# A Mamba and FFN kernel on one core: the DMA queue's engine gets an order of its own, and the lists of all engines are drawn anew

## The chip, the cores and the metric
One core of a Trainium2 chip (trn2). The core has five engines: PE (TensorE), DVE (VectorE), ACT (ScalarE), POOL (GpSimd) and SP (SyncE), which here only issues DMAs. The metric is the time of one execution on the device in microseconds.

## The reference, cut to what matters
Input is x, 8 rows of 1024 tokens with 256 channels. Everything is float32.

```python
def mamba(x, W_in, conv_w, conv_b, W_xproj, W_dt, b_dt, A_log, D_skip, W_out):
    xi, z = split(x @ W_in.T)                      # 512 channels each
    u = silu(causal_conv4(xi, conv_w) + conv_b)
    dt_r, B, C = split(u @ W_xproj.T)              # 16, 16, 16
    dt = softplus(dt_r @ W_dt.T + b_dt)
    A = -exp(A_log)                                # 512 x 16
    # for every channel c and state s, over the tokens of a row:
    #   h[t] = h[t-1] * exp(dt[t] * A) + dt[t] * u[t] * B[t];  y[t] = sum_s h[t] * C[t]
    y = (y + u * D_skip) * silu(z)
    return y @ W_out.T

def ffn(x, w_gate, w_up, w_down):                  # int weights / 127, hidden size 768
    return (silu(x @ w_gate.T) * (x @ w_up.T)) @ w_down.T

x = layernorm(x + mamba(x))
x = layernorm(x + ffn(x))
```

## The kernel before, in words
**Chunks.** The 8 rows of 1024 tokens are cut into 16 chunks of 512 tokens, one after the other; the second half of a row starts from the states that the first half left. In chunk k the core scans the states of chunk k. Beside that it does the *head* of chunk k + 1 (`xi`, convolution, `xproj`, `dt`) and the *tail* of chunk k - 1 (`out`, first normalisation, `x1T`, `gate`, `up`, `down`). The second normalisation and the store are those of chunk k - 2.

**The scan.** A chunk has 64 scans: 4 blocks of 128 channels by 16 states. They are grouped in 16 quads of 4. For each scan ACT makes a decay (`decay_step`, L641), POOL makes a drive for two scans at a time (`drive_unit`, L507: 32 a chunk, from `dtu` and `b_all`), DVE scans (L831). PE transposes the states (L1030, four groups per quad), ACT copies them out (`hT`, L648), and PE multiplies with the diagonals of C and sums (L1044, item `sum`). POOL makes the diagonals (`diag`, L515) from `c_col`. Buffers are few: 3 decays, 4 drives of two scans, 3 quads of states, 2 banks for transposes and 2 banks (`ring`) for all other products. `b_all` and `c_col` have one buffer each, in four parts (g = 0 to 3). A part of `b_all` is free for the next chunk after drives 25, 27, 29 and 31 of this one (counted from 0).

**The order.** Each engine runs its own program in order, and waits on semaphores. Beside the scan's own steps its items stand in a dictionary, `PE_SIDE`, `ACT_SIDE`, `DVE_SIDE`, `POOL_SIDE`. The key (q, j) is a slot: quad q, step j within it (0 to 3; on POOL, 0 and 1, one per drive). ACT's decays are 2 ahead of DVE's scans, and PE transposes in slot (q, j) what quad q - 1 left. Names that matter below: `xi`, `z`, `gate`, `up`: one product of 512 columns; `norm` 0 and 1: four ACT instructions that normalise `res` in place (L699), which need POOL's `std` 0 and 1; `heads` (L528): POOL clears or copies the three columns ahead of `xi` once the convolutions are done; `gate` on POOL: y times silu(z); `x1T`: the transposed input of the FFN; the block of items in ACT's slot (6, 0) needs another table of functions, so a table load stands ahead of it and another behind it (1.28 us each).

**SP.** SP's program has no dictionary. In chunk k it does, in this order: `load_res(k - 1)`; `store(k - 2)`, which waits for `a_o`, counted by `norm` 1; `spread_bc(k + 1)`, which waits for `a_dbl` (ACT's copy of `xproj`), writes B and C to a scratch tensor in memory, waits for that, and loads `c_col` in 16 small DMAs; `load_xt(k + 2)`; then four `load_b(g)`, each behind a wait for its drive. In chunks 0 and 1 there is no store. `b_all` has every row of B on all 128 partitions, 1 MB a part. `xt` and `res` of a chunk are 512 KB each.

Of the kernel before, what the change touches and what calls it, by code (L numbers as in the profile page):

```python
# [48 lines left out]


PE_SIDE = {
    (0, 1): [("xi", 0)], (0, 3): [("sum", 14), ("sum", 15)], (1, 0): [("turn", 3)], (1, 1): [("xi", 1)],
    (1, 2): [("out", 0, 0)], (2, 0): [("out", 0, 1)], (2, 2): [("out", 1, 0)], (3, 0): [("sum", 0)],
    (3, 2): [("out", 1, 1)], (4, 0): [("sum", 1)], (4, 2): [("xi", 2)],
    (5, 0): [("xi", 3), ("z", 0), ("sum", 2), ("sum", 3), ("z", 1), ("z", 2), ("z", 3)],
    (5, 2): [("x1T", 0), ("x1T", 1)], (6, 0): [("turn", 0), ("gate", 0), ("gate", 1)], (6, 2): [("gate", 2)],
    (7, 0): [("sum", 4)], (7, 3): [("up", 0)], (8, 0): [("sum", 5)], (8, 2): [("xproj", 0)],
    (9, 0): [("dt", 0), ("sum", 6), ("sum", 7)], (9, 2): [("up", 1), ("up", 2)], (10, 0): [("gate", 3)],
    (10, 2): [("up", 3)], (11, 0): [("dt", 1), ("sum", 8), ("sum", 9)],
    (11, 2): [("turn", 1), ("gate", 4), ("gate", 5)], (12, 0): [("up", 4)], (12, 1): [("up", 5)],  # L60
    (12, 3): [("sum", 10), ("sum", 11)], (13, 1): [("down", 0, 0), ("turn", 2)], (13, 3): [("down", 0, 1)],
    (14, 1): [("sum", 12)], (14, 3): [("down", 1, 0), ("down", 1, 1)], (15, 3): [("sum", 13)],
}
ACT_SIDE = {
# [16 lines left out]
}  # L81
DVE_SIDE = {
    (1, 2): [("skip", 3)], (4, 2): [("r1", 0)], (5, 0): [("r1", 1)],
    (6, 0): [("conv", 0, 0), ("conv", 0, 1), ("conv", 0, 2), ("conv", 1, 0), ("conv", 1, 1), ("conv", 1, 2), ("conv", 2, 0), ("conv", 2, 1), ("conv", 2, 2), ("conv", 3, 0), ("conv", 3, 1), ("conv", 3, 2), ("skip", 0)],
    (6, 1): [("gs", 0)], (7, 1): [("gs", 1)], (7, 2): [("gs", 2)], (8, 3): [("hid", 0)], (9, 3): [("hid", 1)],
    (10, 0): [("hid", 2)], (10, 3): [("gs", 3), ("hid", 3)], (11, 2): [("skip", 1)], (11, 3): [("gs", 4)],
    (12, 1): [("gs", 5)], (13, 0): [("hid", 4), ("hid", 5)], (14, 1): [("skip", 2)], (14, 3): [("r2", 0)],
    (15, 3): [("r2", 1)],
}
POOL_SIDE = {  # L90
    (2, 1): [("diag", 1), ("gate", 3)], (5, 0): [("diag", 2)], (5, 1): [("diag", 3)], (6, 0): [("std", 0)],
    (6, 1): [("heads", 0)], (7, 0): [("dtu", 1)], (12, 0): [("dtu", 0)], (12, 1): [("std", 1)],
    (13, 0): [("gate", 0)], (15, 1): [("gate", 1), ("gate", 2), ("diag", 0)],
}
PROLOGUE = [("xi", 0), ("xi", 1), ("xi", 2), ("xi", 3), ("xproj", 0), ("dt", 0), ("dt", 1)]
PE_FIRST = PE_LAST = PE_SIDE
ACT_FIRST = ACT_LAST = ACT_SIDE
# [61 lines left out]
def wait(eng, sem, value):  # L159

    if not isinstance(value, int) or value > 0:
        eng.wait_ge(sem, value)
# [39 lines left out]
def banks_of(item):  # L202

    what, i, *part = item
    if what == "dt":
        return [(what, 2 * i), (what, 2 * i + 1)]
    if what == "sum" or what.startswith("end_") or part and part[0] > 0:
        return []
    return [(what, i)]
# [15 lines left out]
def products_in_order(chunks):  # L225

    order = [(what, i, 0) for item in PROLOGUE for what, i in banks_of(item)]
    for c in range(chunks):
# [7 lines left out]
def mamba_ffn(nc, x, xT, W_inT, conv_w, conv_b, W_xT, W_dtT, b_dt, A_log, D_skip, W_outT,  # L236
# [5 lines left out]
    with ExitStack() as ctx:  # L242
        def sb(name, shape, dt=F32):
            return ctx.enter_context(nc.sbuf_tensor(name, shape, dt))
# [27 lines left out]
        xt = sb("xt", [P, 2, DH, T])  # L272
        res = sb("res", [P, 2, TB, DM])
        xi = sb("xi", [P, CB, KW - 1 + T])
        u = sb("u", [P, 2, CB, T])
        dt = sb("dt", [P, 2, CB, T])
        dtu = sb("dtu", [P, CB, T])
        sz = sb("sz", [P, CB, T])
# [6 lines left out]
        hT = sb("hT", [P, HTS, T])  # L285
        yt = sb("yt", [P, T])
        yg = sb("yg", [P, CB, T])
        hid = sb("hid", [P, HB - CB, T])
# [105 lines left out]
        def _(eng):  # L394

            def load_xt(k):
                eng.dma_start(xt[:, k.parity, :, :],
                              xT[:, bass.ds(k.tokens(), T)].rearrange("(a p) t -> p a t", p=P))\
                   .then_inc(l_xt[k.parity], 16)
# [20 lines left out]
            def load_b(g):  # L420
                src = bc_dram[4 * g:4 * g + 4, :].rearrange("(o n) t -> o n t", o=1)
                eng.dma_start(b_all[:, 4 * g:4 * g + 4, :], src.to_broadcast([P, 4, T]))\
                   .then_inc(l_b[g], 16)

            def store(k):
                wait(eng, a_o, k.count(4, 4))
                eng.dma_start(out[bass.ds(k.tokens(), T), :].rearrange("(a p) d -> p a d", p=P),
                              res[:, k.parity, :, :]).then_inc(st_out, 16)

            def load_res(k):  # L430
                wait(eng, st_out, k.count(16, -16))
                eng.dma_start(res[:, k.parity, :, :],
                              x[bass.ds(k.tokens(), T), :].rearrange("(a p) d -> p a d", p=P))\
                   .then_inc(l_res, 16)

            def chunk(k, tail, head, more, late=True):
                if tail:
                    load_res(k + -1)
                if late:
                    store(k + -2)  # L440
                if head:
                    spread_bc(k + 1)
                if more:
                    if tail:
                        wait(eng, p_up, k.count(6, 0))
                    else:
                        wait(eng, p_z, k.count(4, 4))
                    load_xt(k + 2)
                if head:
                    for g in range(4):  # L450
                        wait(eng, g_dr, k.count(32, 24 + 2 * g + 2))
                        load_b(g)

            load_xt(Chunk(0, 0))

# [10 lines left out]
            for half in range(2):  # L466
                chunk(Chunk(0, half), half == 1, True, True, False)
            for row in range(1, ROWS - 1):
                for half in range(2):
                    chunk(Chunk(row, half), True, True, True)  # L470
            for half in range(2):
                chunk(Chunk(ROWS - 1, half), True, half == 0, False)
            kl = Chunk(ROWS - 1, 1)
            load_res(kl)
            store(kl + -1)
            for done, blocks in ((2, slice(0, 2)), (3, slice(2, 3)), (4, slice(3, 4))):
                eng.wait_ge(e_o, done)
# [541 lines left out]
        def _(eng):  # L1019
# [273 lines left out]
            eng.wait_ge(l_in[0], 16)  # L1293
            for what, i in PROLOGUE:
                if (what, i) == ("xi", 1):
# [51 lines left out]
```

## Time and profile before

| | us |
|---|---|
| median of 3 runs | 2083.94 (2083.55 to 2084.12) |
| the profiled execution | 2083.41 |
| its span | 2081.6 |
| PE busy | 1773.4 (85%) |
| DVE busy | 1617.7 (78%) |
| ACT busy | 1617.6 (78%) |
| POOL busy | 1470.6 (71%) |
| mean granted clock of PE | 0.929 of full speed |

The span is from the first to the last instruction in the profile; 1.8 us of the execution lie around it. Busy shares are means over the whole span. PE's weight loads are a group of their own (PEld) and run beside its matmuls. SP's queue entries are issues of DMAs: time between them is SP waiting.

### The profile page before, as it was taken

To read this page: it belongs to the slowest core of one execution; us is meant where nothing else is said; L and a number is where in the kernel's file an instruction comes from. 1 tells how busy PE (TensorE), PEld (TensorE's weight loads), DVE (VectorE), ACT (ScalarE), POOL (GpSimd) and SP (SyncE) were. 2 spreads that over 40 slices of the span, in tenths; PEclk is the share of its full clock that TensorE was granted. 3 is DMA by queue.
4 is the path that set the end of the run, shared out by engine and by line. 5 is a ranking of instruction groups with operands and counts; after the bars stand their busy time and mean duration, and the time that the engine had idled before them with its cause. 6 is when DMAs were issued, how large, how long until landed. Compare 5 with 4: busy or idle time off the path is not lost.

```text
span 2081.6 us, 40418 instructions
## 1 busy us (share of the span) xinstructions
PE 1773.4 (85%) x15806; PEld 1260.1 (61%) x15806; DVE 1617.7 (78%) x1877; ACT 1617.6 (78%) x2792; POOL 1470.6 (71%) x853
## 2 busy tenths in 40 slices
PE   6779998796988969789697896979969699696897
PEld 3556766564665656556565674656756567565676
DVE  5889997795977959689595995959958599586784
ACT  6799897695977959679596895959959599595871
POOL 5788886785857958579584895848868487685860
PEclk8899999898998989999899998989989899898999
DMA  6030301203012030120302103030030300303000
GB/s 183 3 102 3 103 2 13 102 2 113 2 15 100 1 114 1 33 83 2 114 1 63 53 2 114 2 82 33 2 114 1 109 6 13 102 2 104 1 22 21
DMA packets 172146, 100.61 MB, mean 48 GB/s; under 512 B 139538, under 2 KB 158738, under 8 KB 163892
## 3 DMA queue, kind: packets, MB, share of 16 engines
q1 hardware_dynamic: 171956, 98.02, 16.3%
q8 instruction: 126, 2.06, 0.4%
q14 instruction: 64, 0.52, 0.1%
HBM read 88.56 MB, written 9.44 MB: 47 GB/s over the span
## 4 chain that ended last, share of the span: by engine, by line
PE 49%; issue 16%; POOL 11%; ACT 10%; DVE 8%; SPq 4%; DMA 2%; POOLq 0%; ACTq 0%; DVEq 0%
PE ring L1051 14%; PE tp L1030 14%; POOL drive L507 8%; PE yb L1044 8%; PE ring L1149 4%; DVE h L831 4%; PE ring L1125 3%; DVE u L852 3%; SPq L417 3%; ACT hT L648 3%; ACT decay L641 2%; ACT res L699 2%; POOL diag_c L515 2%; ACT u L668 1%; PE ring L1107 1%
## 5 line engine op out<-in xcount | busy, mean ns | idle before, releaser
L507 POOL TENSOR_TENSOR drive<-dtu,b_all 128x1024 f32<-128x1024 f32 x511 | 1201.9, 2378 | 233.0 <-issue 164.0
L641 ACT ACTIVATE decay<-dt,a_neg 128x512 f32<-128x512 f32 x1024 | 688.5, 699 | 263.9 <-DVE h L831 260.7
L831 DVE TENSOR_TENSOR_SCAN h<-decay,h,drive 128x512 f32<-128x512 f32 x512 | 623.5, 1271 | 153.1 <-issue 135.8
L831 DVE TENSOR_TENSOR_SCAN h<-decay,drive 128x512 f32<-128x512 f32 x512 | 594.2, 1212 | 164.8 <-POOL drive L507 121.6
L1030 PE MATMUL tp<-ident,h 128*128 128x128 f32 x4096 | 579.9, 284 | 117.1 <-ACT hT L648 110.8
L1030 PEld LDWEIGHTS tp<-ident,h 128*128 128x128 f32 x4096 | 476.0, 145 | 308.0 <-ACT hT L648 183.8
L648 ACT ACTIVATE hT<-tp 128x512 f32<-128x512 f32 x1024 | 570.9, 601 | 108.7 <-PE tp L1030 107.9
L1051 PE MATMUL ring<-xt,w_in 128*128 128x512 f32 x512 | 261.3, 652 | 142.6 <-DMA xt<-in_xT 140.3
L1044 PE MATMUL yb<-hT,diag_c 128*32 128x128 f32 x8192 | 279.7, 288 | 0.0
L1044 PEld LDWEIGHTS yb<-hT,diag_c 128*32 128x32 f32 x8192 | 228.1, 115 | 49.5 <-issue 38.0
L1051 PEld LDWEIGHTS ring<-xt,w_in 128*128 128x128 f32 x512 | 97.9, 204 | 246.0 <-issue 232.0
L515 POOL TENSOR_TENSOR diag_c<-of_token,c_col 128x512 f32<-128x512 f32 x64 | 67.3, 1052 | 161.0 <-DMA c_col<-bc_scratch 159.4
L1051 PE MATMUL ring<-xt,w_u 128*128 128x512 f32 x360 | 167.8, 595 | 0.0
L1051 PE MATMUL ring<-xt,w_g 128*128 128x512 f32 x360 | 164.4, 593 | 0.0
L852 DVE SCALAR_TENSOR_TENSOR u<-xi,cw,u 128x512 f32<-128x512 f32 x189 | 144.7, 787 | 14.0 <-ACT xi L659 9.6
L1125 PE MATMUL ring<-w_out,yg 128*128 128x256 f32 x480 | 115.4, 384 | 27.4 <-POOL yg L521 27.4
L1149 PE MATMUL ring<-w_d,xi 128*128 128x256 f32 x480 | 113.5, 379 | 0.0
L1125 PEld LDWEIGHTS ring<-w_out,yg 128*128 128x128 f32 x480 | 87.0, 191 | 39.7 <-issue 30.3
L528 POOL TENSOR_TENSOR spare_g<-eps,minus 128x4 f32<-128x4 f32 x17 | 3.4, 200 | 138.7 <-DVE u L852 128.0
L1051 PEld LDWEIGHTS ring<-xt,w_g 128*128 128x128 f32 x360 | 63.7, 190 | 57.4 <-issue 57.4
L1149 PEld LDWEIGHTS ring<-w_d,xi 128*128 128x128 f32 x480 | 87.7, 190 | 10.1
L1051 PEld LDWEIGHTS ring<-xt,w_u 128*128 128x128 f32 x360 | 62.5, 190 | 51.0 <-issue 50.2
(124 smaller groups left out, 1426.1 us busy)
## 6 DMA issues: line engine op xcount, KB each, us to landing
b_all<-bc_scratch SPq DMA_DIRECT2D x63, 1024.0 KB, 9.1
xt<-in_xT SPq DMA_DIRECT2D x16, 512.0 KB, 5.0
res<-in_x SPq DMA_DIRECT2D x16, 512.0 KB, 13.6
out<-res SPq DMA_DIRECT2D x15, 512.0 KB, 3.0
c_col<-bc_scratch SPq DMA_DIRECT2D x256, 2.0 KB, 2.4
bc_scratch<-dbl SPq DMA_DIRECT2D x32, 32.0 KB, 2.4
b_all<-bc_scratch SPq DMA_DIRECT2D x2, 512.0 KB, 4.3
w_g<-in_w_gT SPq DMA_DIRECT2D x1, 768.0 KB
```

Of the source, the lines that this page charges most:

```text
L417: eng.dma_start(c_col[s:P - 3 + s:4, g, :], bc_dram[N + 4 * g + s, :].rearrange("(b t) -> t b", t=TS), allow_slow_non_contiguous=True).the ...
L507: tt(drive[:, j % 4, :, :], src, b_all[:, n:n + 2, :], ALU.mult).then_inc(g_dr, 1)
L515: tt(diag_c[:, g, :, :], mask, col, ALU.mult).then_inc(g_dc, 1)
L641: act(decay[decay_slot(k.parity, i)][:, :], dt[:, k.parity, cb, :], ACT.Exp, scale=a_neg[:, cb, n:n + 1]).then_inc(a_da, 1)
L648: act(hT[:, (64 * k.index + g) % HTS, :], tp[g % 2][:, :], ACT.Copy).then_inc(a_ev, 1)
L831: nc.vector.tensor_tensor_scan(h[:, h_slot(k.parity, q), at:at + T, i % 4], decay[decay_slot(k.parity, i)][:, :], drive[:, (i // 2) % 4, i ...
L852: stt(u[:, k.parity, cb, :], xi[:, cb, tap:tap + T], cw[:, cb, tap:tap + 1], u[:, k.parity, cb, :], ALU.mult, ALU.add).then_inc(v_conv, 1)
L1030: last = nc.tensor.transpose(tp[g % 2][:, b * P:(b + 1) * P], h[:, h_slot(k.parity, q), t0:t0 + TS, :].rearrange("p t s -> p (t s)"), iden ...
L1044: last = mm(yb[b * TS:(b + 1) * TS, f * P:(f + 1) * P], diag_c[:, q % 4, 4 * f + b, :], hT[:, (64 * k.index + g) % HTS, b * P:(b + 1) * P] ...
L1051: last = mm(bank, lhsT, rhs, start=i == 0, stop=i == len(pairs) - 1)
L1125: last = mm(bank(k, "out", i)[:, half * DM:(half + 1) * DM], yg[:, c, tb * P:(tb + 1) * P], w_out[:, c, :], start=c == 0, stop=c == CB - 1)
L1149: last = mm(bank(k, "down", i)[:, half * DM:(half + 1) * DM], hidden_block(m)[:, tb * P:(tb + 1) * P], w_d[:, m, :], start=m == 0, stop=m ...
```

## The change
SP gets an order of its own for a chunk, `SP_ORDER`. The spread of B and C comes first, then three `b_all` loads, then the store, the load of `res`, the fourth `b_all` load and `xt`. `load_res` is now that of chunk k itself, at this place in chunk k, in place of that of k - 1 at the start of the chunk; its wait is for the store just ahead of it. The dictionaries of PE, ACT, DVE and POOL are drawn anew: same items, other slots. `POOL_FIRST`, the first chunk's own list of POOL, stays, as do the lists of the end.

```diff
 PE_SIDE = {
-    (0, 1): [("xi", 0)], (0, 3): [("sum", 14), ("sum", 15)], (1, 0): [("turn", 3)], (1, 1): [("xi", 1)],
-    (1, 2): [("out", 0, 0)], (2, 0): [("out", 0, 1)], (2, 2): [("out", 1, 0)], (3, 0): [("sum", 0)],
-    (3, 2): [("out", 1, 1)], (4, 0): [("sum", 1)], (4, 2): [("xi", 2)],
-    (5, 0): [("xi", 3), ("z", 0), ("sum", 2), ("sum", 3), ("z", 1), ("z", 2), ("z", 3)],
-    (5, 2): [("x1T", 0), ("x1T", 1)], (6, 0): [("turn", 0), ("gate", 0), ("gate", 1)], (6, 2): [("gate", 2)],
-    (7, 0): [("sum", 4)], (7, 3): [("up", 0)], (8, 0): [("sum", 5)], (8, 2): [("xproj", 0)],
...
+    (0, 3): [("xi", 0), ("sum", 14), ("sum", 15), ("xi", 1), ("turn", 3)], (1, 1): [("xi", 2)],
+    (1, 2): [("out", 0, 0)], (2, 0): [("out", 0, 1)], (2, 2): [("xi", 3)], (3, 0): [("sum", 0), ("sum", 1)],
+    (3, 2): [("out", 1, 0)], (4, 0): [("out", 1, 1)], (5, 0): [("sum", 2)], (5, 2): [("z", 0), ("z", 1)],
+    (6, 0): [("z", 2), ("z", 3), ("sum", 3), ("x1T", 0), ("x1T", 1)], (6, 1): [("turn", 0), ("sum", 4)],
+    (6, 3): [("xproj", 0), ("gate", 0), ("gate", 1)], (7, 1): [("gate", 2)], (7, 3): [("sum", 5)],
...
 ACT_SIDE = {
-    (13, 0): [("hT", 48), ("y", 2)], (13, 2): [("hT", 49)], (13, 3): [("hT", 50)],
-    (14, 2): [("hT", 51), ("hT", 52), ("hT", 53)], (14, 3): [("hT", 54), ("norm", 1)],
...
+    (6, 0): [("sz", 0), ("sz", 1), ("norm", 0), ("hT", 19), ("sz", 2), ("u", 0), ("sz", 3), ("u", 1), ("y", 0), ("x1T", 0), ("u", 2), ("hT", 20), ("hT", 21), ("x1T", 1), ("u", 3)],
+    (6, 3): [("xproj", 0), ("hT", 22), ("hT", 23), ("tanh", 0)],
...
+    (13, 0): [("y", 2), ("hT", 48), ("hT", 49)], (13, 1): [("hT", 50), ("hT", 51)], (13, 3): [("norm", 1)],
...
 POOL_SIDE = {
-    (2, 1): [("diag", 1), ("gate", 3)], (5, 0): [("diag", 2)], (5, 1): [("diag", 3)], (6, 0): [("std", 0)],
-    (6, 1): [("heads", 0)], (7, 0): [("dtu", 1)], (12, 0): [("dtu", 0)], (12, 1): [("std", 1)],
-    (13, 0): [("gate", 0)], (15, 1): [("gate", 1), ("gate", 2), ("diag", 0)],
+    (1, 1): [("diag", 1)], (3, 0): [("gate", 3)], (4, 0): [("diag", 2)],
+    (6, 1): [("std", 0), ("diag", 3), ("heads", 0)], (7, 1): [("dtu", 1)], (10, 0): [("std", 1)],
+    (11, 0): [("dtu", 0)], (13, 1): [("gate", 0)], (14, 0): [("gate", 1)], (15, 0): [("gate", 2)],
+    (15, 1): [("diag", 0)],
 }
+SP_ORDER = [("spread", 0), ("bload", 0), ("bload", 1), ("bload", 2), ("store", 0), ("res", 0), ("bload", 3), ("xt", 0)]
...
-            def chunk(k, tail, head, more, late=True):
-                if tail:
-                    load_res(k + -1)
-                if late:
+            def item(k, what, i, tail, head, more, late):
+                if what == "res":
+                    load_res(k)
+                if what == "store" and late:
                     store(k + -2)
-                if head:
+                if what == "spread" and head:
                     spread_bc(k + 1)
-                if more:
+                if what == "xt" and more:
                     if tail:
                         wait(eng, p_up, k.count(6, 0))
                     else:
                         wait(eng, p_z, k.count(4, 4))
                     load_xt(k + 2)
-                if head:
-                    for g in range(4):
-                        wait(eng, g_dr, k.count(32, 24 + 2 * g + 2))
-                        load_b(g)
+                if what == "bload" and head:
+                    wait(eng, g_dr, k.count(32, 24 + 2 * i + 2))
+                    load_b(i)
+
+            def chunk(k, tail, head, more, late=True):
+                for what, i in SP_ORDER:
+                    item(k, what, i, tail, head, more, late)
...
-            load_res(kl)
             store(kl + -1)
```

DVE's list changes too: the twelve convolution steps, all in slot (6, 0) before, now stand as five in (5, 3) and seven in (6, 0).

## Rows read from the trace of the kernel before

**Rows 1.** The waits: engine and line, awaited; us in total, times, longest.
```profile
POOL drive L507 <- issue: 164.0, 13, 13.1
POOL diag_c L515 <- DMA c_col<-bc_scratch: 159.4, 13, 12.8
PE ring L1051 <- DMA xt<-in_xT: 140.3, 12, 12.7
...
PE ring L1125 <- POOL yg L521: 27.4, 14, 2.7
```

**Rows 2.** The waits of SP's own queue.
```profile
SPq L427 <- ACT res L699: 1589.6, 15, 112.4
```

**Rows 3.** Timeline of ACT at a boundary: start, us, instructions, idle before.
```profile
991.87 2.06 ACT L699 ACTIVATE res<-res,shift,rstd 128x256 f32<-128x256 f32 x4
```

**Rows 4.** Timeline of SP at the same boundary.
```profile
993.96 0.39 SPq L427 DMA_DIRECT2D out<-res  x1
...
997.37 10.73 SPq L417 DMA_DIRECT2D c_col<-bc_scratch  x16
1008.14 0.62 SPq L397 DMA_DIRECT2D xt<-in_xT  x1
1008.81 2.13 SPq L422 DMA_DIRECT2D b_all<-bc_scratch  x4
```

**Rows 5.** Timeline of POOL at the same boundary.
```profile
987.37 2.51 POOL L521 TENSOR_TENSOR yg<-yg,sz 128x512 f32<-128x512 f32 x2
1001.85 1.04 POOL L515 TENSOR_TENSOR diag_c<-of_token,c_col 128x512 f32<-128x512 f32 x1 [11.96 <-DMA c_col<-bc_scratch]
1015.79 14.00 POOL L507 TENSOR_TENSOR drive<-dtu,b_all 128x1024 f32<-128x1024 f32 x6 [12.89 <-issue]
```

**Rows 6.** Timeline of PE at the same boundary.
```profile
1013.33 3.75 PE L1051 MATMUL ring<-xt,w_in 128*128 128x512 f32 x4 [11.00 <-DMA xt<-in_xT]
1020.74 1.97 PE L1030 MATMUL tp<-ident,h 128*128 128x128 f32 x8 [3.66 <-ACT hT L648]
```

**Rows 7.** Timeline of PE at the boundary from chunk 1 to chunk 2.
```profile
251.74 1.88 PE L1051 MATMUL ring<-xt,w_in 128*128 128x512 f32 x4
253.46 1.04 PE L1030 MATMUL tp<-ident,h 128*128 128x128 f32 x8
```

**Rows 8.** Busy time in one stretch: PE, PEld, DVE, ACT, POOL, PE's clock, DMA share, GB/s.
```profile
1010.00:1018.00 8.00, 3.75 (x4) 1.17 (x4) 0.00 (x0) 0.00 (x0) 2.21 (x1) 0.50 0.99 386
```

**Rows 9.** Timeline of SP at the boundary from chunk 1 to chunk 2.
```profile
205.19 11.04 SPq L417 DMA_DIRECT2D c_col<-bc_scratch  x16
...
229.00 8.68 SPq L422 DMA_DIRECT2D b_all<-bc_scratch  x4
```

**Rows 10.** Busy time as in rows 8, of two whole chunks.
```profile
184.90:291.70 106.80, 105.19 (x985) 75.37 (x984) 99.98 (x117) 98.93 (x172) 90.51 (x49) 1.00 0.19 52
...
993.96:1122.29 128.33, 109.95 (x985) 77.79 (x985) 98.88 (x117) 101.15 (x176) 91.67 (x52) 0.92 0.16 47
```

**Rows 11.** POOL's spare_g instruction of heads: ns min/median/max, first and last start.
```profile
L528 POOL TENSOR_TENSOR spare_g<-eps,minus x17: 198/200/204, 3.7 to 1834.1; 128x4 f32<-128x4 f32 x17
```

**Rows 12.** DVE's scans in the page's costliest groups: busy, mean ns, idle before.
```profile
L831 DVE TENSOR_TENSOR_SCAN h<-decay,drive 128x512 f32<-128x512 f32 x512 | 594.2, 1212 | 164.8 <-POOL drive L507 121.6
```

**Rows 13.** Timeline of POOL at the boundary from chunk 1 to chunk 2.
```profile
232.46 4.87 POOL L507 TENSOR_TENSOR drive<-dtu,b_all 128x1024 f32<-128x1024 f32 x2 [1.15 <-DVE h L831]
...
241.85 9.35 POOL L507 TENSOR_TENSOR drive<-dtu,b_all 128x1024 f32<-128x1024 f32 x4
```

**Rows 14.** DMA issues: count, KB each, median us from issue to landing.
```profile
out<-res SPq DMA_DIRECT2D x15, 512.0 KB, 3.0
```

**Rows 15.** Timeline of ACT: the table loads around the block of slot (6, 0).
```profile
1054.31 1.28 ACT L673 ACT_TABLE_LOAD   x1
...
1065.76 1.28 ACT L641 ACT_TABLE_LOAD   x1
```

**Rows 16.** Timeline of PE: the xproj product.
```profile
1077.84 1.95 PE L1088 MATMUL ring<-u,w_x 128*64 128x256 f32 x16
```

More of the change, by code:

```diff
@@ L58 @@
[L58 to L62, printed above, removed]
+    (0, 3): [("xi", 0), ("sum", 14), ("sum", 15), ("xi", 1), ("turn", 3)], (1, 1): [("xi", 2)],
@@ new lines @@
+    (1, 2): [("out", 0, 0)], (2, 0): [("out", 0, 1)], (2, 2): [("xi", 3)], (3, 0): [("sum", 0), ("sum", 1)],
+    (3, 2): [("out", 1, 0)], (4, 0): [("out", 1, 1)], (5, 0): [("sum", 2)], (5, 2): [("z", 0), ("z", 1)],
+    (6, 0): [("z", 2), ("z", 3), ("sum", 3), ("x1T", 0), ("x1T", 1)], (6, 1): [("turn", 0), ("sum", 4)],
+    (6, 3): [("xproj", 0), ("gate", 0), ("gate", 1)], (7, 1): [("gate", 2)], (7, 3): [("sum", 5)],
+    (8, 1): [("up", 0)], (8, 3): [("dt", 0), ("sum", 6), ("sum", 7)], (9, 1): [("up", 1), ("up", 2)],
@@ L63 @@
+    (9, 3): [("gate", 3)], (10, 1): [("up", 3)], (10, 3): [("sum", 8)], (11, 1): [("dt", 1)],
+    (11, 3): [("sum", 9), ("sum", 10)], (12, 1): [("gate", 4), ("gate", 5)], (12, 2): [("turn", 1)],
+    (12, 3): [("up", 4), ("up", 5), ("sum", 11)], (13, 1): [("turn", 2)],
+    (13, 3): [("down", 0, 0), ("down", 0, 1)], (14, 1): [("sum", 12)], (14, 3): [("down", 1, 0)],
+    (15, 1): [("down", 1, 1)], (15, 3): [("sum", 13)],
 }
 ACT_SIDE = {
[16 rows of a table removed]
[16 rows of a table added]
 }
 DVE_SIDE = {
-    (1, 2): [("skip", 3)], (4, 2): [("r1", 0)], (5, 0): [("r1", 1)],
@@ L84 @@
[L84 to L87, printed above, removed]
@@ L88 @@
-    (15, 3): [("r2", 1)],
+    (1, 2): [("skip", 3)], (3, 2): [("r1", 0)], (5, 0): [("r1", 1)],
+    (5, 3): [("conv", 0, 0), ("conv", 0, 1), ("conv", 0, 2), ("conv", 1, 0), ("conv", 1, 1)],
+    (6, 0): [("conv", 1, 2), ("conv", 2, 0), ("conv", 2, 1), ("conv", 2, 2), ("conv", 3, 0), ("conv", 3, 1), ("conv", 3, 2)],
+    (6, 1): [("skip", 0)], (7, 1): [("gs", 0)], (7, 3): [("gs", 1), ("gs", 2)], (8, 2): [("hid", 0)],
+    (9, 2): [("hid", 1)], (9, 3): [("hid", 2)], (10, 2): [("gs", 3)], (11, 0): [("hid", 3)],
@@ L89 @@
+    (12, 0): [("gs", 4), ("gs", 5), ("skip", 1)], (12, 3): [("hid", 4), ("hid", 5)], (13, 2): [("skip", 2)],
+    (14, 2): [("r2", 0)], (15, 3): [("r2", 1)],
 }
 POOL_SIDE = {
-    (2, 1): [("diag", 1), ("gate", 3)], (5, 0): [("diag", 2)], (5, 1): [("diag", 3)], (6, 0): [("std", 0)],
-    (6, 1): [("heads", 0)], (7, 0): [("dtu", 1)], (12, 0): [("dtu", 0)], (12, 1): [("std", 1)],
-    (13, 0): [("gate", 0)], (15, 1): [("gate", 1), ("gate", 2), ("diag", 0)],
+    (1, 1): [("diag", 1)], (3, 0): [("gate", 3)], (4, 0): [("diag", 2)],
```

27 rows, old and new, of the table ACT_SIDE are left out of this document.

## The prediction
> **What bounds the kernel now.** I read the waits first, then the timelines of the engines around the largest of them, then the busy time of whole chunks. The list of waits has three groups that come once per chunk, and their counts and sizes match: POOL's `diag_c` waits 12 us for `c_col` from the DMA, 13 times; right after it POOL's drive sits idle another 12.6 us, 13 times ("issue", a wait that the profile does not attribute); PE's first input product waits 11.7 us for `xt`, 12 times [rows 1]. The queue's own waits say who holds them: SP stands at line 427, the store, waiting for ACT's second normalisation, 15 times and 1590 us in all [rows 2]. Line 427 is ahead of everything else that SP does in a chunk.
>
> At one boundary it reads so. ACT's four `res` instructions end at 993.93 [rows 3]; SP issues the store at 993.96 and only then the rest: 16 `c_col` issues in 10.7 us, `xt` at 1008.14, the four `b_all` from 1008.81 [rows 4]. POOL has finished the chunk's last drive at 987.4 and its gates at 989.9, gets `c_col` at 1001.85 and `b_all` at 1015.79 [rows 5]. So POOL loses 12.0 + 12.9 = 24.9 us. DVE and ACT run dry behind it, PE waits for `xt` until 1013.33 and is back on transposes only at 1020.74; the product then takes 3.75 us, where it takes 1.88 in the other boundary [rows 6, 7], because the granted clock of that stretch is 0.50, the lower of the two levels [rows 8].
>
> The same kernel shows a boundary without this. Chunks 0 and 1 have no store, so the spread of chunk 1 for chunk 2 went out at 205.19 and the `b_all` loads at 229.00, as drives set them free [rows 9]. From chunk 1's `heads` (184.9) to chunk 2's (291.7) it takes 106.8 us, with PE 105.19 us busy (98.5%) at a granted clock of 1.00, DVE 99.98, ACT 98.93, POOL 90.51; a later chunk takes 128.33 with PE 109.95 at 0.92 [rows 10]. The `heads` of chunks 2 and 14 (the last of 17) are at 291.7 and 1834.1, 12 periods: 128.53 us each [rows 10, 11]. This pair is the core of the forecast: without the SP stall PE is the bound, at 105.2 us a chunk, and the work of all engines fits in 106.8.
>
> **The change, part by part.** (1) *SP's order.* The spread now waits for `a_dbl` alone, which ACT gives in slot (6, 3). Its issues take about 14 us (10.7 for `c_col`, some 3.4 for the scratch writes and their landing [rows 4]), and are done long before POOL's (15, 1). The loads 0 to 2 wait for drives 25, 27 and 29. The two POOL waits, 24.9 us, go. None of this is extra work: the number of DMAs is the same, only their order changes.
>
> (2) *What now stands behind the store.* The store waits for `norm` 1, then `load_res` waits for the store's landing, and behind these two stand the fourth `b_all` load and `xt`. Which is late next? In the old chunk ACT's norm ended 6.6 us after POOL's last drive (993.93 against 987.4 [rows 3, 5]), from slot (14, 3). It moves to (13, 3), four decays earlier; each decay follows a scan of about 1.2 us [rows 12], so I put its end 1.7 us after the last drive. I lay that on the boundary without stall, where the last drive ended at 237.3 [rows 13]: norm 239.0, store issued 0.4 later, landed 3.0 after that [rows 14], 242.4. Behind it `res`, `b_all` and `xt` are 2.1 MB; at the 386 GB/s that the loads reached [rows 8] 5.4 us, and the store's 3.0 us less its own 1.4 us of bytes leaves 1.6 us of latency. With half a microsecond of issue, `xt` lands at about 250.0. The product that needs it started at 251.74 there, in slot (0, 1) [rows 7]; the new lists put it at (0, 3), two groups of transposes (0.5 us each [rows 7]) further on. Taking 252 to 253, 2 to 3 us are to spare: cost 0. If the cover is gone the cost is the lateness itself, on PE, 13 times. The last `b_all` is first needed in POOL's seventh drive, 14 us into the chunk: no cost.
>
> One rule speaks against this step. The Trainium skill, "DMA: Bandwidth & Descriptors", gives under "Anatomy of one DMA" a fixed 2.0 us and bytes over 436 GB/s, and under "Bandwidth" a limit of some 358 GB/s between one core and its memory. By the first `xt` would land at 242.9 + 2.0 + 4.8 = 249.7, by the second at 250.8. It makes a wait for a completed write ahead of loads cost its full latency, and the trace bears out the size of that (3.0 us [rows 14]); both results are still ahead of 252.
>
> (3) *The lists.* The work per engine is unchanged: PE 105.2, ACT 98.9 plus the second norm's 2.06 [rows 3], DVE 100, POOL 90.5. So the floor of a chunk is 105.2, and what counts is the idle time of PE. Two new places: the `xi` products now come early, so the block of Silu work in ACT's (6, 0) finds PE with little in stock. ACT's block took 12.7 us from its table load to the end of the load back [rows 15]. PE has in (6, 0) to (6, 3) four products (1.7 each), `xproj` (1.9), four groups of transposes, `x1T`, a turn and two sums (about 5 together): 13.8 us [rows 7, 16]. The last `gate` waits for ACT's copy of `xproj`, which stands behind the block and three decays, about 17.5 us after the start: 3.7 us of PE idle. Second, `out` 0 waits in (1, 2) for POOL's `gate` 3, which moves from after the sixth to after the seventh drive; PE already waits 2.0 us a time there (27.4 over 14 [rows 1]), and I reckon 1.9 for it and for `xi` 2 behind ACT's copy of `xi` 1. If PE had no backlog anywhere, a chunk would be 105.2 + 3.7 + 1.9 = 110.8. If it always had, 105.2. The old lists without a stall made 106.8, the nearest row. PE has the most work of the four engines (105.2 against at most 101), so it runs behind the others for much of a chunk and can fill a wait from its backlog; I count half of the two waits: 105.2 + 2.8 = **108.0 us**. Ends for the range: 105.5 and 112.
>
> **Sum.** Twelve periods: 12 x (128.53 - 108.0) = 246.4. The thirteenth boundary, into the last chunk, has no `xt` and stalls about 2.2 us less: 18.3. The period from chunk 1 to 2 gets 1.2 longer (108.0 against 106.8). Chunk 0, the last chunk and the end keep their work; I count 0 with 4 us either way, since the last chunk is already a chunk with little to fill it. 2083.4 (the profiled execution's own time, 0.5 below the median of 2083.94) less 263.5: **1820 us**.
>
> **The rivals.**
> *The new lists fit worse.* PE idle grows beyond both waits counted, say a chunk of 112: 12 x 16.5 + 14.3 - 5.2 = 207, 1876 us. For it: ACT has 101 us of work in the chunk with both normalisations, and its long block stands where the `xi` stock is gone. Against: no engine has over 105.2, and lists of this kind reached 106.8. Chance 0.11.
> *A new wait takes the place of the old.* `xt` arrives late behind store, `res` and `b_all`. If norm ends as late as before (6.6 us after the last drive) it lands near 255, 2 to 3 us late; with PE's restart at the low clock after it, 5 us a boundary, chunks of 113: 12 x 15.5 + 13.3 - 6.2 = 193, 1890 us. Chance 0.07.
> *Slower than before.* Same place, with a longer chain: `norm` needs POOL's `std` in (10, 0), the store needs `norm`, `res` needs the store, PE's `xi` needs `xt`. It decides when `xt` is later than PE's need by more than 128.5 - 108 = 20.5 us a chunk, when the store would have to be some 23 us later than reckoned; at 24 us, 1820 + 13 x 24 = 2132 us. Nothing in the rows delays it so; `std` 1 has its input since the chunk's start. Chance 0.02.
> *The change doesn't do what it says.* The POOL idle labelled "issue" might be another limit; but it ends as `b_all` lands, and at the boundary where SP was free the drive goes on at 241.85, 4.5 us after the last one with two gates and `diag_c` between [rows 5, 13]. No gain, 2083: chance 0.01.
> *The clock.* PE nearly always busy could be granted less than now. The unstalled chunk ran at 1.00 for all of its 106.8 us [rows 10], so I add nothing; the mean should rise from 0.93.
>
> **How the numbers follow.** The forecast (chunks of 105.5 to 110.5, 1784 to 1855) has 0.79; worse lists 0.11, late `xt` 0.07, slower 0.02, no change 0.01. A range of 1788 to 1866 leaves out the last three, half of the worse lists and a little at the lower end. About 0.2% (4 us) is what a measurement of this kernel can tell from no change. Faster 0.97, within 0.2% 0.01, slower 0.02.
>
> **What would show it right or wrong.** `heads` 106 to 111 us apart; no wait of `diag_c` for `c_col`, no idle of the drive over 2 us at the boundary; SP's `c_col` issues in mid chunk and its long wait now ahead of `b_all` or the store; PE's clock near 1.00 outside the first and last chunk; PE over 95% busy; short PE waits for ACT around the Silu block. Wrong: a wait of PE's input product for `xt` of over 1 us each chunk (second rival), or ACT more than 97% busy with PE under 94% (first).

## The result, and the profile after

| | before | after |
|---|---|---|
| median, us | 2084.03 (4 runs) | 1803.8 (4 runs, 1801.26 to 1804.67) |
| ratio, 95% interval | | 0.8654 (0.8639 to 0.8669) |
| span of the profiled execution, us | 2081.6 | 1803.0 |
| mean granted clock of PE | 0.929 | 0.983 |

The forecast was 1820 us with a range of 1788 to 1866. The page of the changed kernel, its busy times and the shares of the chain that ended last:

```profile
span 1803.0 us, 40418 instructions
PE 1727.5 (96%) x15806; PEld 1230.6 (68%) x15806; DVE 1603.5 (89%) x1877; ACT 1620.4 (90%) x2792; POOL 1473.2 (82%) x853
...
PE 73%; DVE 9%; ACT 8%; issue 6%; POOL 4%; SPq 0%; DMA 0%; POOLq 0%; ACTq 0%; DVEq 0%
```

The same shares in the kernel before:

```profile
PE 49%; issue 16%; POOL 11%; ACT 10%; DVE 8%; SPq 4%; DMA 2%; POOLq 0%; ACTq 0%; DVEq 0%
```

SP and the DMAs, 6% of the chain before, are gone from it. In the list of waits the three that came once per chunk [rows 1] have no successor. What the same instructions still wait for is other engines, little at a time (total us, times, longest); the first row is the longest total among the scan's own waits, the last one is PE's wait for `gate` 3 on POOL, which the forecast had counted in every chunk:

```profile
DVE h L836 <- ACT decay L646: 87.9, 58, 4.7
POOL drive L512 <- DVE h L836: 71.9, 41, 11.0
...
POOL diag_c L520 <- PE yb L1049: 9.2, 14, 0.7
...
PE ring L1130 <- POOL yg L526: 6.5, 2, 4.7
```

SP's own waits, where the 1590 us at the store [rows 2] are now spread over several places, the largest one for `a_dbl` in mid chunk:

```profile
SPq L407 <- ACT dbl L686: 831.5, 16, 61.1
SPq L425 <- POOL drive L512: 451.0, 47, 17.2
SPq L430 <- ACT res L704: 188.8, 15, 100.0
SPq L435 <- DMA out<-res: 39.8, 14, 3.5
```

One boundary in SP's timeline (L425 is a `b_all` load, L430 the store, L435 `res`, L400 `xt`, L420 `c_col`; compare [rows 4]):

```profile
990.23 0.39 SPq L430 DMA_DIRECT2D out<-res  x1
993.16 0.38 SPq L435 DMA_DIRECT2D res<-in_x  x1
993.58 0.51 SPq L425 DMA_DIRECT2D b_all<-bc_scratch  x1
994.13 0.43 SPq L400 DMA_DIRECT2D xt<-in_xT  x1
1049.68 0.79 SPq L407 DMA_DIRECT2D bc_scratch<-dbl  x2
1051.62 10.80 SPq L420 DMA_DIRECT2D c_col<-bc_scratch  x16
1079.52 14.26 SPq L425 DMA_DIRECT2D b_all<-bc_scratch  x3
```

The same boundary on POOL, where [rows 5] had 12.0 and 12.9 us of idle:

```profile
990.26 2.39 POOL L512 TENSOR_TENSOR drive<-dtu,b_all 128x1024 f32<-128x1024 f32 x1
993.35 1.05 POOL L520 TENSOR_TENSOR diag_c<-of_token,c_col 128x512 f32<-128x512 f32 x1 [0.70 <-PE yb L1049]
994.36 7.02 POOL L512 TENSOR_TENSOR drive<-dtu,b_all 128x1024 f32<-128x1024 f32 x3
```

On PE the first `xi` product starts with no wait and at full clock (1.88 us where [rows 6] have 3.75):

```profile
1004.40 1.88 PE L1056 MATMUL ring<-xt,w_in 128*128 128x512 f32 x4
```

Two whole chunks in busy time (PE, PEld, DVE, ACT, POOL, clock, DMA share, GB/s), to set against [rows 10]:

```profile
937.80:1044.70 106.90, 106.16 (x1004) 75.59 (x1008) 98.61 (x117) 101.68 (x177) 91.78 (x52) 1.00 0.20 56
1044.70:1151.30 106.60, 105.47 (x979) 74.70 (x972) 99.34 (x117) 100.97 (x175) 91.83 (x52) 1.00 0.20 57
```

The `heads` of the first and last full period, as [rows 11]: the last one starts at 1578.2, that of chunk 2 at 297.49 in POOL's timeline.

```profile
L533 POOL TENSOR_TENSOR spare_g<-eps,minus x17: 200/202/752, 3.7 to 1578.2; 128x4 f32<-128x4 f32 x17
```

(1578.2 - 297.49) / 12 = 106.73 us a chunk, where it was 128.53. So the 278.6 us of the span come in three parts: 12 x 21.8 = 261.6 from the twelve periods; 22.7 from the last boundary to the end (1803.0 - 1578.2 = 224.8, before 2081.6 - 1834.1 = 247.5); and 5.8 lost up to the `heads` of chunk 2 (297.49 against 291.68). All of that loss lies before the `heads` of chunk 1 (190.74 against 184.88); from there to chunk 2 both kernels take the same, 106.75 and 106.80 us.

### The profile page after: what moved, and what is told of

Same layout as the page of the kernel before. It is cut to its first block, busy times and chain, and to the rows that moved or that the text cites. A ratio compares the mean times of both kernels' runs of the same rounds, so it can differ in the third digit from the quotient of the medians.

```text
span 1803.0 us, 40418 instructions
## 1 busy us (share of the span) xinstructions
PE 1727.5 (96%) x15806; PEld 1230.6 (68%) x15806; DVE 1603.5 (89%) x1877; ACT 1620.4 (90%) x2792; POOL 1473.2 (82%) x853
## 4 chain that ended last, share of the span: by engine, by line
PE 73%; DVE 9%; ACT 8%; issue 6%; POOL 4%; SPq 0%; DMA 0%; POOLq 0%; ACTq 0%; DVEq 0%
PE ring L1056 25%; PE tp L1035 20%; PE yb L1049 11%; PE ring L1130 6%; DVE h L836 6%; PE ring L1154 4%; ACT hT L653 3%; POOL drive L512 3%; PE ring L1112 2%; PE ring L1093 2%; ACT L646 1%; ACT L693 1%; ACT decay L646 1%; DVE u L857 1%; ACT dt L693 1%
## 5 line engine op out<-in xcount | busy, mean ns | idle before, releaser
L653 ACT ACTIVATE hT<-tp 128x512 f32<-128x512 f32 x1024 | 562.7, 602 | 60.2 <-PE tp L1035 57.8
L1035 PE MATMUL tp<-ident,h 128*128 128x128 f32 x4096 | 566.1, 280 | 34.5 <-ACT hT L653 32.2
L1035 PEld LDWEIGHTS tp<-ident,h 128*128 128x128 f32 x4096 | 465.6, 143 | 189.7 <-ACT hT L653 82.6
L1049 PE MATMUL yb<-hT,diag_c 128*32 128x128 f32 x8192 | 265.6, 276 | 2.3 <-ACT hT L653 2.2
L1049 PEld LDWEIGHTS yb<-hT,diag_c 128*32 128x32 f32 x8192 | 212.9, 110 | 64.5 <-issue 47.5
L1056 PE MATMUL ring<-xt,w_in 128*128 128x512 f32 x512 | 241.7, 607 | 1.6 <-ACT dt L693 0.9
L1056 PEld LDWEIGHTS ring<-xt,w_in 128*128 128x128 f32 x512 | 91.6, 193 | 89.6 <-issue 84.6
L526 POOL TENSOR_TENSOR yg<-yg,sz 128x512 f32<-128x512 f32 x63 | 80.7, 1282 | 0.0
```

Source lines behind the costliest of these rows:

```text
L526: tt(yg[:, cb, :], yg[:, cb, :], sz[:, cb, :], ALU.mult).then_inc(g_y, 1)
L653: act(hT[:, (64 * k.index + g) % HTS, :], tp[g % 2][:, :], ACT.Copy).then_inc(a_ev, 1)
L1035: last = nc.tensor.transpose(tp[g % 2][:, b * P:(b + 1) * P], h[:, h_slot(k.parity, q), t0:t0 + TS, :].rearrange("p t s -> p (t s)"), iden ...
L1049: last = mm(yb[b * TS:(b + 1) * TS, f * P:(f + 1) * P], diag_c[:, q % 4, 4 * f + b, :], hT[:, (64 * k.index + g) % HTS, b * P:(b + 1) * P] ...
L1056: last = mm(bank, lhsT, rhs, start=i == 0, stop=i == len(pairs) - 1)
```

## The experiments

All ratios are to the kernel before, run beside it on the same chip. The period is read as above, from the `heads` of chunks 2 and 14 in each trace.

| run | us | ratio, 95% interval | heads, chunk 2 and 14 | us a chunk |
|---|---|---|---|---|
| before | 2084.03 | | 291.68, 1834.1 | 128.5 |
| the change | 1803.8 | 0.8654 (0.8639 to 0.8669) | 297.49, 1578.2 | 106.7 |
| e1, SP's order, old lists | 1860.56 | 0.8927 (0.8914 to 0.8941) | 293.58, 1631.0 | 111.5 |
| e2, old SP, new lists | 2055.6 | 0.9863 (0.9849 to 0.9878) | 296.52, 1812.2 | 126.3 |
| e3, store last, old lists | 1799.02 | 0.8631 (0.8617 to 0.8645) | 294.12, 1573.0 | 106.6 |
| e4, spread first, old lists | 1915.44 | 0.9195 (0.9179 to 0.9212) | 293.37, 1679.4 | 115.5 |
| e5, the change, store last | 1803.92 | 0.8649 (0.8637 to 0.8661) | 296.72, 1577.5 | 106.7 |
| e6, the change, old first chunk | 1800.73 | 0.8634 (0.8623 to 0.8646) | 293.95, 1574.7 | 106.7 |
| c1, the change again | 1803.74 | 0.8649 (0.8637 to 0.8661) | 297.68, 1578.4 | 106.7 |
| c2, e3 again | 1799.65 | 0.8631 (0.8619 to 0.8643) | 291.64, 1570.9 | 106.6 |
| e9, xt later, 2 copies | 1848.78 | 0.8866 (0.8837 to 0.8896) | 293.93, 1617.8 | 110.3 |
| e10, xt later, 5 copies | 1962.84 | 0.9404 (0.9388 to 0.9419) | 311.15, 1736.1 | 118.7 |
| e11, gate half | 1806.88 | 0.8665 (0.8652 to 0.8677) | 298.42, 1579.8 | 106.8 |
| e12, store from ACT, old lists | 1807.47 | 0.8663 (0.865 to 0.8676) | 291.42, 1579.6 | 107.3 |

### Which part of the change brings it: e1 to e4

**e1** is the changed kernel with the four dictionaries of before.

```diff
-PE_SIDE = {  (0, 3): [("xi", 0), ("sum", 14), ...        # likewise ACT, DVE, POOL
+PE_SIDE = {  (0, 1): [("xi", 0)], (0, 3): [("sum", 14), ...
```

> SP's new order with the four dictionaries of before. Theory A (the gain is SP's order; the old lists without a stall made 106.8 us a chunk, as from chunk 1 to 2 in the kernel before): POOL's two boundary waits go. But the old norm 1 in slot (14, 3) ends 6.6 us after POOL's last drive and the old first xi product in (0, 1) wants xt about 14.4 us after it; store landing 3.0, issues about 1.3 and the 7.7 us to landing that xt has in the changed kernel make 18.6, so xt is some 4 us late and a restart of PE is added: 106.8 + 5 = 112 us a chunk, about 1870 us. Theory B (the lists carry a large part of the gain, at least a third): over 1900 us.

1860.56 us and 111.5 us a chunk: theory A, to a half per cent. This is also the prediction's second rival, met with the old lists: 4.9 us a chunk over e3, for the 5 that were put on a late `xt`. The lateness of `xt` is there; the wait is 3.3 us a time (expected 4):

```profile
PE ring L1054 <- DMA xt<-in_xT: 40.0, 12, 4.5
```

and at one boundary PE starts after it at the lower clock again, 3.75 us for the product that takes 1.88 otherwise:

```profile
1031.71 3.75 PE L1054 MATMUL ring<-xt,w_in 128*128 128x512 f32 x4 [3.48 <-DMA xt<-in_xT]
```

**e2** is the kernel before with the new dictionaries, SP untouched.

> SP as before (residual, store, spread, xt, four b_all), with the new dictionaries. Theory A: the stall stays, but norm 1 comes from slot (13, 3), some 4.9 us earlier against POOL's last drive than from (14, 3), so each of 13 boundaries stalls that much less: about 2084 - 13 x 5 = 2020 us, POOL still waiting about 8 us for c_col and then for b_all. Theory B: the new lists hold a good part of the gain by themselves, under 1960 us.

Neither number came. The lists alone bring 28 us. `diag_c` does wait 6.0 us less each time (81.6 over 13, before 159.4 over 13), which is what norm 1's earlier slot should give, but most of that is lost again on PE. Its waits:

```profile
POOL diag_c L517 <- DMA c_col<-bc_scratch: 81.6, 13, 7.5
PE ring L1053 <- DMA xt<-in_xT: 67.9, 12, 6.8
...
PE ring L1127 <- POOL yg L523: 59.5, 14, 6.6
PE ring L1118 <- ACT yt L666: 54.1, 14, 13.0
```

The two last rows have grown: `out` waits 4.3 us a time for `yg`, 2.0 in [rows 1], and `turn` 3.9 us for `yt`. In the new lists the first `xi` product stands ahead of the last two sums, so whatever waits for the sums (`yt`, `turn`, the skip, `gate` 3, `out`) now also waits for `xt`. That reading is from the order of the items and the two rows; no run moved `xi` alone, so it is not shown.

**e3** is the kernel before with one edit.

```diff
 def chunk(k, tail, head, more, late=True):
     if tail:
         load_res(k + -1)
-    if late:
-        store(k + -2)
     if head:
         spread_bc(k + 1)
...
             load_b(g)
+    if late:
+        store(k + -2)
```

> The kernel before with one edit: the store moves from ahead of the spread to the end of SP's chunk. No new lists, the residual stays first. Theory A: nothing needed soon stands behind the store any more, chunks take the 106.8 us of the unstalled one plus up to 1.5 for the second normalisation: 1800 to 1825 us. Theory B (the new lists are needed): over 1850 us.

1799.02 us, just under theory A's window of 1800 to 1825, and no slower than the whole change. So the gain needs neither the new lists nor the new place of the residual; it needs the store out of the way. SP's timeline of one chunk: the spread in mid chunk, `xt` and the four parts of B as drives release them, then a wait of 6 us for the store that nobody else stands behind.

```profile
1058.43 11.89 SPq L417 DMA_DIRECT2D c_col<-bc_scratch  x16
1083.21 0.40 SPq L397 DMA_DIRECT2D xt<-in_xT  x1
1083.65 8.70 SPq L422 DMA_DIRECT2D b_all<-bc_scratch  x4
1098.55 0.39 SPq L427 DMA_DIRECT2D out<-res  x1
1102.40 0.38 SPq L432 DMA_DIRECT2D res<-in_x  x1
```

**e4** moves only the spread ahead of the store; `xt` and B's parts stay behind it.

```diff
+    if head:
+        spread_bc(k + 1)
     if late:
         store(k + -2)
-    if head:
-        spread_bc(k + 1)
     if more:
```

> The kernel before with the spread of B and C ahead of the store, but xt and the four b_all loads still behind it. Splits the stall in its parts. Theory A (two stalls in series, c_col and then b_all): c_col is there in time, xt and b_all are issued 1.6 us after the end of norm 1, so drives restart about 14 us after the last one where they did after 28.4, and after 4.5 in the boundary without stall: about 116 us a chunk, 1925 us, no wait of diag_c for c_col, and a drive idle of 8 to 10 us each boundary. Theory C (c_col alone is what holds the boundary, b_all and xt are hidden behind it): about 1815 us.

115.5 us a chunk for 116 expected: two stalls in series, about 13 us of the 22 a chunk from C's columns and 9 from B's parts and `xt`. `diag_c` no longer waits for a DMA, and the drive still does:

```profile
1043.62 1.05 POOL L515 TENSOR_TENSOR diag_c<-of_token,c_col 128x512 f32<-128x512 f32 x1 [1.11 <-PE yb L1044]
1055.35 13.97 POOL L507 TENSOR_TENSOR drive<-dtu,b_all 128x1024 f32<-128x1024 f32 x6 [10.68 <-issue]
```

### Whether it is the order on one queue: e12

**e12** leaves SP's order alone and takes the stores off it.

```diff
 def normalise(k, norm):                    # on ACT
     for tb in range(TB):
         act(res[:, k.parity, tb, :], ...).then_inc((a_x1, a_o)[norm], 1)
+    if norm:
+        wait(eng, a_o, k.count(4, 4))
+        eng.dma_start(out[bass.ds(k.tokens(), T), :]..., res[:, k.parity, :, :]).then_inc(st_out, 16)
...
 def chunk(k, tail, head, more, late=True):  # on SP
     if tail:
         load_res(k + -1)
-    if late:
-        store(k + -2)
...
-            store(kl + -1)
```

> The kernel before with nothing of SP's order changed but the stores taken off it: ACT issues each store itself, right after its second normalisation. Old lists. Theory A (what cost the time was only that the spread and all behind it stood behind a wait for norm 1 on one queue): the same gain as from the store at the end, 1798 to 1812 us, ACT's issue of about half a microsecond a chunk hidden. Theory I (the loads collide with the store's transfer, wherever it is issued): over 1850 us.

1807.47 us, theory A. The store's transfer at its old place in the order, right behind norm 1, costs nothing that shows; what cost was the wait in SP's program ahead of everything else. The issue on ACT's queue:

```profile
1098.92 2.06 ACT L696 ACTIVATE res<-res,shift,rstd 128x256 f32<-128x256 f32 x4
1101.02 0.38 ACTq L700 DMA_DIRECT2D out<-res  x1
```

One part of the expectation missed: the issue isn't hidden. A chunk takes 107.3 us where e3 and c2 take 106.6. In ten of the twelve periods the granted clock is 1.00 and a chunk takes 107.0 us on average, half a microsecond more. That is about what the issue costs ACT, which goes from the start of norm 1 to its next decay in 2.5 us where it took 2.0 in e3. In the two others the clock is 0.98 and a chunk takes 108.9, and these make the rest.

### What is left at the boundary: e5, e9, e10

**e5**: `SP_ORDER` ends with the fourth `b_all` load, `xt`, store, `res`.

> The changed kernel with the store and the residual moved behind the fourth b_all and xt. Theory A (PE is the bound at 106.7 us a chunk, and xt already lands about 2 us ahead of its use): no change, 1800 to 1806 us. Theory D (the wait for the store's landing ahead of xt still costs something each chunk): at least 1 us a chunk less, under 1792 us.

No change: 1803.92 us, and 1803.74 for the changed kernel run beside it (c1).

**e9 and e10** put two and five copies of 128 KB in memory, each waited for, ahead of every `xt` load.

```diff
+    for _ in range(2):                     # e10: 5
+        eng.dma_start(pad[:, :], x[0:P, :]).then_inc(st_pad, 16)
+        pads[0] += 16
+        eng.wait_ge(st_pad, pads[0])
     load_xt(k + 2)
```

> The changed kernel with two small copies in memory (128 KB each, each waited for, some 2 us) ahead of every xt load. In the changed kernel xt is issued at 888.27, lands 7.7 us later and is used at 897.93: some 2 us to spare. Theory A (that is all the cover there is): 14 boundaries are 2 to 3 us late, 1803.8 + 28 to 42 = 1832 to 1846 us, and PE waits for xt appear. Theory G (PE's backlog or a shorter landing absorbs it): under 1812 us.

> The same with five copies ahead of every xt load, some 10 us. Theory A (lateness counts one for one once the 2 us are used, and PE restarts at the lower clock): 8 us late plus 1 to 3 us for the clock at 14 boundaries, 1930 to 1960 us, granted clock down to about 0.95. Theory G (half of it is absorbed): under 1890 us. This prices the second rival of the prediction, a late xt.

Both landed a little above theory A's windows, because the copies take SP longer than the 2 us each that I put. One alone does land 2.3 to 2.4 us after its issue, but the first of them is issued behind `res` and the `b_all` part in flight and lands after 6.9 us (both in e10, from 1077.95 on). SP's timeline of e9, then of e10:

```profile
1010.84 0.51 SPq L427 DMA_DIRECT2D b_all<-bc_scratch  x1
1011.39 7.31 SPq L454 DMA_DIRECT2D pad_scratch<-in_x  x2
1020.50 0.38 SPq L402 DMA_DIRECT2D xt<-in_xT  x1
```

```profile
1077.95 14.57 SPq L454 DMA_DIRECT2D pad_scratch<-in_x  x5
1094.32 0.38 SPq L402 DMA_DIRECT2D xt<-in_xT  x1
```

The issue of `xt` moves by 9.1 and 16.4 us. But with `res` and the `b_all` part no longer in flight ahead of it, `xt` lands 3.7 us after its issue, not 7.7, so it is 5.1 and 12.4 us later. Chunks grow by 3.6 and 12.0 us. PE's waits, e9 and e10 (the 35.8 are over 13, 2.8 us each; the 129.7 over 14, 9.3 each):

```profile
PE ring L1062 <- DMA xt<-in_xT: 35.8, 13, 5.0
```

```profile
PE ring L1062 <- DMA xt<-in_xT: 129.7, 14, 10.9
```

So about 2 to 3 us of lateness are covered (5.1 less 2.8, 12.4 less 9.3), and beyond that a microsecond costs a microsecond, plus 0.8 (e9) and 2.7 us (e10) a chunk. In e9 the granted clock accounts for the 0.8: six of the twelve periods ran at 1.00 and took 109.3 us on average, 2.6 over the changed kernel; the other six ran at 0.98 and took 111.3. In e10 the late product itself runs at a granted clock of 0.50 (1098 to 1101 in its trace), and the mean of the execution is 0.946. Theory G is out.

### Where the first two chunks lose: e6, c1, c2

**e6** gives the first chunk the old lists of PE, ACT and DVE; `PE_FIRST`, `ACT_FIRST` and `DVE_FIRST` are the dictionaries of before.

> The changed kernel, with PE's, ACT's and DVE's lists of before in the first chunk alone. The changed kernel reaches the heads of chunk 2 at 297.49 us where the one before is at 291.68, the only place where it lost. Theory A (the new lists leave the first chunk, with POOL's list unchanged, worse matched): 3 to 6 us come back, 1798 to 1801 us. Theory E (the loss is in the change-over to the second chunk, whose lists are then still the new ones): within 2 us of the changed kernel, and heads of chunk 2 still near 297.

> The changed kernel as it is, on the same chip as the other runs of this call: 1801 to 1806 us under every theory.

> The kernel before with the store at the end of SP's chunk, on the same chip as the changed kernel. Theory A (both are bound by PE in the steady chunks, and differ by the 3 to 6 us of the first two chunks): 1797 to 1801 us, 3 to 6 below the changed kernel. Theory F (the first difference of 4.8 us was one between chips): within 1.5 us of it.

e6 takes 1800.73 us (1800.47 to 1801.19), c1 beside it 1803.74 (1803.38 to 1804.69): 3.0 us back, and the `heads` of chunk 2 come 3.7 us earlier. The loss sits between the `heads` of chunk 0 and of chunk 1. That stretch takes 104.3 to 104.8 us in the five runs with the new lists and `xt` in time, 99.6 to 101.8 in the six with the old lists, and 101.0 in e6. So the first chunk's lists carry most of the loss, perhaps all of it. How much is not settled to better than 2 us, since e3 and c2, the same kernel, differ by 2.5 us at the `heads` of chunk 2, and e9, with the new lists, took 102.7 for that stretch, which is unexplained. That POOL's list, not drawn anew, is what they fit badly is argued; no run changes it. c2 takes 1799.65 us against c1's 1803.74, 4.1 less: theory A as to the time, and the old lists with the store last are at least as good as the change. Their intervals against the kernel before overlap; the executions themselves do not (1798.89 to 1802.29 and 1803.38 to 1804.69). No version tried beats e3.

### Whether PE is the bound: e11

**e11** leaves out the second 128 of 256 channels in the `gate` products (all chunks but the end), so it no longer computes the layer; its time alone is of use.

```diff
 product(to[:, :], [(weight[:, d, m * P:(m + 1) * P], x1[:, d, :])
-                   for d in range(DH)], done)
+                   for d in range(1 if weight is w_g else DH)], done)
```

> The changed kernel with PE's work cut: the gate products leave out the second half of their contraction (128 of 256 channels) in all chunks but the end. It takes 6 x 0.86 = 5.2 us of PE's work off a chunk; DVE, ACT and POOL keep theirs. Theory A (PE alone is the bound; the next is ACT with 101 us a chunk): 3 to 5 us a chunk less, 1730 to 1760 us. Theory H (the engines are bound together through the few buffers, ACT no less than PE): under 1.5 us a chunk, over 1780 us.

Theory A falls. With 5.2 us of PE's work gone from each chunk (the estimate of the expectation; PE's busy time fell by 3.7 to 3.9) the mean period is 106.8 us, as before it, and the time 1806.88 us. The shares of the chain that ended last moved from PE (73% in the changed kernel, with ACT at 8%) to ACT above all:

```profile
PE 44%; ACT 28%; DVE 12%; issue 11%; POOL 3%; DMA 1%; SPq 1%; ACTq 0%; POOLq 0%; DVEq 0%
```

The mean of 106.8 hides two kinds of period. Nine of the twelve ran at a granted clock of 1.00 and took 106.4 us on average, 0.3 less than in the changed kernel. The other three ran at 0.98 and took 107.9. One of each:

```profile
1152.80:1259.10 106.30, 102.17 (x992) 72.93 (x988) 98.49 (x117) 101.37 (x177) 91.80 (x53) 1.00 0.20 57
1259.10:1366.90 107.80, 103.19 (x966) 73.15 (x962) 99.57 (x117) 100.72 (x175) 91.82 (x52) 0.98 0.19 56
```

So the rival that the lower clock ate a real gain is answered by the first kind: at full clock the missing work brings 0.3 us a chunk, not 3 to 5. The two differences offset each other in the sum. Theory H's figures hold (under 1.5 us a chunk, over 1780 us); its reason, that the few buffers bind the engines together, is not shown.

Cut into slices of 8.9 us, a period of the changed kernel suggests how this can be: different engines are full in different slices. One slice right after the Silu block and one at the next boundary, in the columns as above. In the first ACT is busy throughout (8.87) and DVE is not (7.99); in the second ACT is at 7.00 and DVE at 8.50, PE full in both. The second block has the same two stretches in e11:

```profile
1151.30:1160.20 8.90, 8.90 (x74) 5.42 (x71) 7.99 (x9) 8.87 (x16) 8.74 (x6) 1.00 0.04 7
...
1204.70:1213.60 8.90, 8.90 (x82) 7.82 (x81) 8.50 (x13) 7.00 (x13) 8.20 (x5) 1.00 0.76 282
```

```profile
1152.80:1161.70 8.90, 7.95 (x72) 4.65 (x65) 7.98 (x9) 8.87 (x17) 8.76 (x6) 1.00 0.04 9
...
1206.20:1215.10 8.90, 8.90 (x82) 7.82 (x80) 8.34 (x13) 6.79 (x13) 8.21 (x5) 1.00 0.74 271
```

The work was taken where ACT is full too; at the boundary PE is as full as before. So e11 shows that the `gate` products don't set the period, and leaves open whether PE does so elsewhere. e12's half microsecond a chunk for a short issue on ACT fits with ACT being on the path. Which items of ACT, DVE or PE (outside `gate`) set the 106.7 is open: no run took work off them.

## Why the prediction was right, by its steps

- **SP at the store is the stall** (first part): right, and shown by e3, which moves nothing but the store. e4 gives the two parts of it, 13 and 9 us a chunk.
- **The boundary from chunk 1 to 2 as the measure of a chunk without stall**: right. It gave 106.8, the changed kernel takes 106.73 and e3 106.6. This was the best evidence in the trace; the forecast would have been closer had it stayed with it.
- **What stands behind the store costs 0**: right. Norm 1 came even earlier than put (the store is issued at 990.23, the last drive ends at 992.65), `xt` was issued at 994.13 and landed some 7.7 us later, near 1001.8 with PE needing it at 1004.40. From the point that the forecast put at 242.9 to the landing it had 7.1 us, and 8.1 came; the earlier norm 1 made up for that. The cover of 2 to 3 us is what e9 and e10 measure. The margin was thin, as e1 shows: with norm 1 and `xi` in the old slots the same order of SP costs 4.9 us a chunk more than e3. What the new lists do is fit this order of SP; with the store last there is nothing to fit.
- **Two new PE waits, half of them counted, 2.8 us a chunk**: the mis-sized term. PE is idle 0.7 to 1.1 us in a period. The wait of `out` for `gate` 3, put at up to 1.9 with the one behind `xi` 1, is 6.5 us in the whole run, over 2 times; the 3.7 us in the Silu block did not come, PE being busy there for 29.75 of the 30 us from 1130 to 1160. PE had the backlog for the whole of the two waits, where the forecast took half, a share that no row gave. 1.27 us a chunk too many is 15.2 us over the twelve periods, nearly all of the 16 between forecast and result.
- **"Without the SP stall PE is the bound"**: not borne out as an account, though its number held. e11 takes 5.2 us off PE and a chunk at full clock gets 0.3 us shorter. The sum did not need the statement, since the 106.8 were measured with all engines in them; the floor of 105.2 did, and the lower end of the range with it.
- **First chunks and the end**: 1.2 us were added for the period from chunk 1 to 2 and nothing for chunk 0. That period stayed as it was (106.75), and 5.9 us were lost ahead of it, 3.0 of them in the first chunk's lists by e6's time. The last boundary gave 22.7 where 18.3 were put: it stalled no less than the others (21.8), and the 2.2 us taken off it had no row. One miss is 4.6 us, the other 4.4 the other way; that they cancel is luck.
- **The clock**: right. Chunks run at 1.00, and the mean is 0.983 for 0.929.
- **The Trainium skill's two figures for `xt`** (the Trainium skill, "DMA: Bandwidth & Descriptors": under "Anatomy of one DMA" the fixed cost with 436 GB/s, which is a fit for DMAs issued by GpSimd, and under "Bandwidth" 358 GB/s): they gave 6.8 and 7.9 us from the point put at 242.9, half a microsecond after the store's landing. From the same point in the changed kernel (993.7) to the landing near 1001.8 it is 8.1 us, near the second sum. The rate itself is not borne out: the loads reached 386 GB/s [rows 8], so the agreement is in the sum alone.
- **The rivals**: worse lists did not happen in steady chunks. A late `xt` did not happen in the change, and did in e1. Neither of the last two, slower and no gain, happened.

## What to carry to other kernels

A DMA queue's engine runs its program in order: a wait that is long and harmless for its own transfer (a store of an old result) holds every load written behind it, here for some 22 us a chunk (128.5 before, 106.6 in e3). Put such a wait behind the loads that are needed next, or on another queue, before drawing any schedule anew; here one moved wait did the same as a new order for SP and new lists for four engines. Look for a stretch of the same trace where the suspected wait is absent and read the gain from there, but don't take the busiest engine for the bound until work taken off it makes a difference, and read the clock of each period before comparing means.

## What the runs showed of the hardware

- How long a load takes from issue to landing depends on what is in flight ahead of it on the queue: `xt` (512 KB) 7.7 us (median) behind `res` and a 1 MB part of B in the changed kernel, 3.7 us in e9 and e10 with both already landed. The 4.0 us between them for 1.57 MB are 393 GB/s, near the 386 of [rows 8].
- A copy of 128 KB from memory to memory lands 2.3 to 2.4 us after its issue when nothing is ahead of it, and 6.9 us after it behind `res` and a part of B (e10, four copies and the first one). A 512 KB store takes 2.9 us to its landing (median in the changed kernel).
- PE shows 99% busy in a chunk of the changed kernel, and an estimated 5.2 us of its products could go for 0.3 us of time at full clock (e11); its busy time fell by less than that, by 3.7 to 3.9 us.
- Somewhat more idle time of PE at the boundary can lower its clock, and need not. In e11 PE was busy 2.32 of the 4.00 us from 868 to 872, and in the next four the granted clock was 0.59, with the lower level (0.50) in part of them. Such a fall came in three of e11's twelve periods, two of e12's, six of e9's and none of the changed kernel's, and a period with it was 1.3 to 2 us longer than one without.
